# Forty bytes of padding ahead of the large SBUF tensors of a fused attention and mixture-of-experts kernel

## The reference

```
xn = layernorm(x)
# attention branch, over all 4096 tokens
q = xn @ Wq;  v = xn @ Wv                      # 1024 x 1024 each
s[t] = sigmoid(beta) * s[t-1] + v[t]           # a linear scan along each sequence, by head
y = layernorm(q * s) * ln_g + ln_b
y = (y * silu(xn @ Wg)) @ Wo
# expert branch: 64 experts, top 8 of them for each token
p = softmax(xn @ router_w.T); (w, e) = top_k(p, 8); w = w / sum(w)
for each expert with up to 128 of its tokens xg:
    h = silu(xg @ w1.T) * (xg @ v1.T)          # 384 hidden features
    ffn[token] += w * (h @ w2)
out = x + y + ffn
```

## Time and profile before

| | |
|---|---|
| median of three runs | 2539.49 us |
| lowest and highest | 2534.47 and 2539.74 us |
| the profiled execution's own time | 2539.86 us |
| its span, first to last instruction | 2538.2 us |
| mean granted TensorE clock | 0.992 |
| TensorE (PE) busy | 2493.7 us, 98%, 13,649 matmuls |
| VectorE (DVE) / ScalarE (ACT) / GpSimd (POOL) busy | 64% / 52% / 27% |
| DMA | 605.74 MB, mean 239 GB/s |

### The profile page before, as it was taken

How to read it: one execution, slowest core, us unless ns; L and a number is a source line. 1 busy time by engine, 2 the same in 40 slices (tenths; PEclk the granted TensorE clock), 3 DMA queues, 4 the chain that set the end, 5 groups by cost and what they waited for, 6 DMA issues and landing times.

```text
span 2538.2 us, 39295 instructions
## 1 busy us (share of the span) xinstructions
PE 2493.7 (98%) x13649; PEld 2214.3 (87%) x13649; DVE 1629.1 (64%) x1689; ACT 1320.7 (52%) x1499; POOL 674.5 (27%) x523
## 2 busy tenths in 40 slices
PE   7999999999999999999999999999999999999997
PEld 6888978898889988899888998889988889988896
DVE  7776897666666665666566666656666566656654
ACT  5566323554446644556445565445654456544554
POOL 3221122223322232322223222322223222323211
PEclk9999999999999999999999999999999999999999
DMA  8785854897668966779766797765986669866686
GB/s 278 260 301 193 240 189 162 257 306 228 191 224 254 312 215 217 228 234 295 239 228 204 227 316 249 224 217 197 311 277 191 224 217 284 276 217 228 207 268 162
DMA packets 151790, 605.74 MB, mean 239 GB/s; under 512 B 20592, under 2 KB 37040, under 8 KB 151216
## 3 DMA queue, kind: packets, MB, share of 16 engines
q1 hardware_dynamic: 116304, 518.91, 57.1%
q0 software_dynamic: 35424, 86.00, 16.5%
HBM read 520.89 MB, written 100.70 MB: 245 GB/s over the span
## 4 chain that ended last, share of the span: by engine, by line
PE 93%; DVE 3%; DMA 2%; ACT 1%; issue 1%; POOL 0%; SPq 0%; ACTq 0%; DVEq 0%; POOLq 0%
PE psA L1543 18%; PE psA L1545 18%; PE psA L1544 18%; PE psH L1543 7%; PE psH L1545 7%; PE psH L1544 7%; PE psY L1543 4%; PE psY L1545 4%; PE psY L1544 3%; PE psX L1650 2%; PE psY L1575 2%; PE psX L1670 1%; DMA ew_raw<-ew_dram 1%; DMA xn_turned<-xraw 1%; PE psH L1689 1%
## 5 line engine op out<-in xcount | busy, mean ns | idle before, releaser
L1156 DVE TENSOR_TENSOR ew_lo<-ew_raw,ew_hi 128x1536 fp32r<-128x1536 f32 x384 | 693.9, 1816 | 340.1 <-ACT ew_hi L752 326.0
L752 ACT ACTIVATE ew_hi<-ew_raw 128x1536 fp32r<-128x1536 f32 x384 | 568.4, 1484 | 163.0 <-DMA ew_raw<-ew_dram 128.5
L1543 PE MATMUL psA<-xT_hi,pw_hi 128*128 128x512 f32 (+1 forms) x1544 | 621.3, 402 | 3.5 <-DVE xT_lo L1073 2.9
L746 ACT ACTIVATE pw_hi<-pw_raw 128x1024 fp32r<-128x1024 f32 x254 | 266.4, 1060 | 674.2 <-PE psA L1545 671.7
L1545 PE MATMUL psA<-xT_hi,pw_lo 128*128 128x512 f32 (+1 forms) x1544 | 610.5, 395 | 0.0
L1544 PE MATMUL psA<-xT_lo,pw_hi 128*128 128x512 f32 (+1 forms) x1544 | 606.8, 393 | 0.0
L1151 DVE TENSOR_TENSOR pw_lo<-pw_raw,pw_hi 128x1024 fp32r<-128x1024 f32 x256 | 313.8, 1236 | 161.5 <-ACT pw_hi L746 156.1
L1543 PE MATMUL psH<-ew_hi,gT_hi 128*128 128x384 f32 x1024 | 352.7, 344 | 0.8
L1545 PEld LDWEIGHTS psA<-xT_hi,pw_lo 128*128 128x128 f32 x1544 | 292.4, 189 | 69.8
L1544 PEld LDWEIGHTS psA<-xT_lo,pw_hi 128*128 128x128 f32 x1544 | 294.9, 191 | 63.5
L1543 PEld LDWEIGHTS psA<-xT_hi,pw_hi 128*128 128x128 f32 x1544 | 291.5, 189 | 64.9 <-issue 4.7
(11 more groups left out here) (161 smaller groups left out, 3342.3 us busy)
## 6 DMA issues: line engine op xcount, KB each, us to landing
ew_raw<-ew_dram SPq DMA_DIRECT2D x384, 768.0 KB, 6.3
pw_raw<-proj_w_dram SPq DMA_DIRECT2D x256, 512.0 KB, 5.2
xn_scratch<-xt SPq DMA_DIRECT2D x33, 512.0 KB, 4.6
xt<-x_dram SPq DMA_DIRECT2D x32, 512.0 KB, 6.0
out_dram<-x_dram SPq DMA_DIRECT2D x32, 512.0 KB, 5.7
out_dram<-ot POOLq DMA_DIRECT2D x32, 512.0 KB, 12.4
xn<-xn_turned SPq DMA_DIRECT2D x29, 512.0 KB, 4.1
xn_turned<-xraw SPq DMA_DIRECT2D x28, 512.0 KB, 5.1
```

Source lines behind the costliest of these rows:

```text
L746: act.activation(dst[:, slot, :, :], pw_raw[:, slot, :, :], ACT.Copy).then_inc(s_pwhi, 1)
L752: act.activation(ew_hi[:, c % 3, :], ew_raw[:, c % 3, :], ACT.Copy).then_inc(s_ewhi, 1)
L1156: dve.tensor_tensor(ew_lo[:, c % 3, :], ew_raw[:, c % 3, :], ew_hi[:, c % 3, :].bitcast(F32), ALU.subtract).then_inc(s_ewlo, 1)
L1543: pe.matmul(dst, l_hi, r_hi_, start=first, stop=False)
```

## The change

One line is added between the small tensors and the large ones. It rounds the absolute address of the next tensor up to a multiple of 128 bytes: 18,392 becomes 18,432, and every tensor placed after it lies 40 bytes higher than before.

```
--- before.py
+++ after.py
@@ -104,6 +104,7 @@
         col = place("col", [P, 6, NT], F32)
         col_hi = place("col_hi", [P, 2, NT], F32R)
         half = place("half", [P, 4], F32)
+        top[0] = -(-(top[0] + slab_at) // 128) * 128 - slab_at
         xT_hi = place("xT_hi", [P, KC, TB], F32R)
         xT_lo = place("xT_lo", [P, KC, TB], F32R)
         at_y = top[0]
```

## The result

The padded kernel takes 2492.97 us, the median of four runs (2492.13 to 2499.34), against 2538.47 us for the kernel before (four runs, 2534.47 to 2539.74). The ratio is 0.983, with a 95% interval of 0.981 to 0.985: 1.7% faster, 45.5 us. Forecast was no change, 2538.0 us, with a range of 2526 to 2545.

A forecast was written before the change was run, and what follows sets the result against it. TensorE was taken as the bound: number of matmuls times distance between starts. Profiled 2539.86 us - 1.5 (starts) - 0 (other engines) - 0 (DMA) = 2538.4; the runs' median lies 0.37 lower, so 2538.0 us, range 2526 to 2545.

The forecast's parts named there:

- Shorter transfers: Rival on DMA: loads and stores lose a ragged end, 2 us at 0.3 us a landing; over 5 us faster: chance 0.04.
- The slower rival: Turns read tile and `ident` at the same remainder and collide: 2548 us at 10 ns each, 2592 at 53; chance 0.13.
- That DMA traffic has little part in the distances: 256-column matmuls: DMA shares of 0.01 and 1.09 gave 123.3 and 122.8 ns, so DMA writes cost TensorE nothing.
- TensorE's part: Matmul streams: 14,952 starts of runs at 0.1 ns each, 1.5 us gained; far end 1.0 ns, 15.0 us.
- the near end: Lowest price of a misaligned start in the matmul streams: 0, read from the half-clock matmuls that showed no surcharge.
- A bound of 1.0 ns on a further start: 256 columns in two runs: one more misaligned start costs 0.8 ns, 1.0 taken as far end, 15.0 us over all starts.
- the 426.7 ns at 1.2 GHz: Last expert's output at half clock: 512 columns take just their bare time, read as no cost per misaligned start.
- this rival: The matmuls' surcharge is the misalignment: slope part 67.7 us gives 2472 us, all of it 2320; chance 0.04 (below 2480).
- A block costs: Matmul runs each save one 128-byte block at 0.44 ns: 6.6 us, 2531.5 us; chance 0.17 together with a start costing.
- the working's 0 for VectorE: VectorE's instructions: no gain or loss counted, 0 us, since their waiting for TensorE covers any change.

The follow-up runs named there:

- r32: Padded kernel with all large tensors shifted to begin 32 bytes past a multiple of 128; 512 columns came to 226.7 ns, its total time is not in the text.
- r64: Padded kernel with all large tensors shifted to begin 64 bytes past a multiple of 128; 226.7 / 173.3 / 120.0 ns, its total time is not in the text.

## Why the prediction was wrong

**What held.** TensorE's distance sets the time, and the gain comes from it; no other term brought any. ScalarE's splits (1,484 and 1,059 ns), VectorE's and the turns stayed, as forecast. "Shorter transfers" did not occur: the loads of `pw_raw` and `xt` land after 5.3 and 6.0 us, where it was 5.2 and 6.0, and the store of `xt` to its scratch after 4.7, where it was 4.6. The slower rival, turns that meet `ident` at the same remainder, did not occur either: turns have a median distance of 109 ns in both traces. That DMA traffic has little part in the distances fits both traces: between the quarter of stretches of 12 matmuls with the most DMA traffic and the quarter with the least they differ by 1.0 ns at most, in both directions.

**The step that failed** is the one under "TensorE's part": "nothing is paid per start that the slower columns do not cover, and the near end is 0. I take 0.1 ns a start". It had 1.5 us, measured are 61.2 us in steady distances and 47.0 in the span. Three things were wrong in it.

First, the price was sought per misaligned start, by comparing one run with two runs in the same kernel. But what a ragged placement costs is neither per start nor per operand: it is a slower pace of the whole stream, 16 cycles of 2.4 GHz at 512 columns (6.7 ns), and it differs by form. Both forms that I compared had it, so their difference could not show it. A bound of 1.0 ns on a further start is no bound on the loss that all of them share.

Second, the 426.7 ns at 1.2 GHz were taken as a clean control. The kernel after has the same 426.7. The half clock hides the effect, it does not price it. The row itself could have warned: it showed none of the 20.0 ns that the same form had over its columns at full clock, and 13.3 of those are still there with the padding.

Third, the row that spoke up was there: 0.4305 ns a column where the clock gives 0.4167. The working named it, put 67.7 us on it (2472 us) and gave it 0.04, with the argument that a shift by some bytes cannot change the number of full blocks. That is an argument from a picture of the reads, against a measured slope that nothing else explained. The slope is now 0.4167, so this rival had the right term: the part that grows with the columns went, the constant 13.3 ns stayed. Of its 67.7 us, 61.2 showed up in steady distances; the rest lies within the rounding of the rows. Its time of 2472 us did not come, since of these 61.2 only 47 reached the span. "A block costs" (2531.5 us) looked at the same slope and took a seventeenth of it. It is refuted by the size, and by r32 and r64, where each run enters one 128-byte block more and is as quick as aligned.

**What the working left out** are the two things that took 14 us back. About 7 us went because the quick pace is only reached some matmuls after each interruption. Another 7 us went into longer gaps, of which 4.1 us are TensorE's waits for the experts' weights: the working's 0 for VectorE, with its waiting for TensorE as the cover, left out that at these 25 places TensorE waits for VectorE, before (7.3 us) and more so now (11.4 us). The rest of the longer gaps was not traced to a cause.

## What to carry to other kernels

Compare the distance between matmuls with their columns at the granted clock, over two sizes: a slope above one column per cycle is time that something takes, and a chance to be tested, not explained away. A row of idle time understates a wait on an engine whose instructions overlap; take the distance between the starts. For float32r operands in SBUF try places before you reason about them: both operands at a multiple of 32 bytes and a multiple of 256 bytes apart was the quick one for 384 and 512 columns here, and the traces show within one run whether a stream has it. A control is only a control if the effect could have shown in it.

## What was not expected of the hardware

- The pace of a matmul stream at full clock depends on the starts of both operands together. For 512 columns: 226.7 ns (both at 0, 32 or 64, a multiple of 256 apart), 231.0 (both at 16), 232.0 (128 apart), 233.0 (32 apart), 233.3 (16 apart, both at 8, or one or both at 88). For 384: 173.3, also with the stationary operand 32 or 88 off; 175.7 with both at 16, 176.3 with the stationary one 16 off, 176.7 with 128 between them; 180.0 with only the moving one at 88. For 256 in two runs of 128: 117.0 to 119.7 where the operands are 16, 32 or 128 apart, 118.0 where both are at 16, 120.0 when aligned and also with one of the two at 88, 123 when both are at 8 or 88.
- The quick pace has to be found: after an interruption the first matmuls of 512 and 384 columns are slower, for five to ten matmuls (0.70, 0.69, 0.68 us for three).
- A subtraction of VectorE that began during a 1.30 us addition of GpSimd took 2.71 us instead of 1.76, in 24 of 24 cases; no run tested the cause.
- 13.3 ns, 32 cycles of 2.4 GHz, stay over the columns at the best alignment of 384 and 512. At 384 columns they do not go with the number of weights. What they are, and by which rule the reads of the two operands get in each other's way, stays open; that the reads collide at all is argued from the dependence on the distance, not shown.
